# Two feed-forward weights made ternary on GpSimd instead of VectorE, in a gated cross-attention block

## What is computed

```python
def act_quant(x):
    scale = 127.0 / jnp.clip(jnp.max(jnp.abs(x), axis=-1, keepdims=True), 1e-05)
    return jnp.clip(jnp.round(x * scale), -128, 127) / scale
def weight_quant(w):
    scale = 1.0 / jnp.clip(jnp.mean(jnp.abs(w)), 1e-05)
    return jnp.clip(jnp.round(w * scale), -1, 1) / scale
def bit_linear(x, w):                       # value of: act_quant(x) @ weight_quant(w).T
...
h = bit_linear(x, w1)                       # 256 -> 1024
h = depthwise_conv1d(h, conv_w, conv_b)     # three taps along the sequence
return bit_linear(jax.nn.silu(h), w2)       # 1024 -> 256
...
x = x + tanh(g_xattn) * xattn(layernorm(x), ctx, ctx, Wq, Wk, Wv, Wo)
x = x + tanh(g_ffn)   * ffn(layernorm(x), w1, conv_w, conv_b, w2)
```

## Time and profile before

| what | value |
|---|---|
| median of 3 runs | 236.85 us (235.79 to 237.44) |
| span of the profiled execution | 235.2 us |
| TensorE busy in the span | 215.8 us (92%) |
| VectorE busy | 190.4 us (81%) |
| ScalarE busy | 161.9 us (69%) |
| GpSimd busy | 122.2 us (52%) |

### The profile page before, as it was taken

The page is one execution under the profiler, slowest core; times in us unless marked ns, Lnnn a source line. Parts: engine busy times, 40 slices in busy tenths (PEclk is TensorE's granted clock), DMA queues, the critical chain, the costliest instruction groups (busy, mean ns, idle before and its releaser), DMA issues.

```text
span 235.2 us, 6424 instructions
## 1 busy us (share of the span) xinstructions
PE 215.8 (92%) x2439; PEld 180.1 (77%) x2452; DVE 190.4 (81%) x387; ACT 161.9 (69%) x318; POOL 122.2 (52%) x229
## 2 busy tenths in 40 slices
PE   7999999997999999999999999989985699997974
PEld 7887787886878787887878878768783588886963
DVE  4163548789798999999999999999899859999671
ACT  2557768777687888989889788667933356674741
POOL 2421326364365757668677576657567224433470
PEclk9999999999999999999999999999999589999999
DMA  5982011010110101100000000000000000111111
GB/s 168 370 270 67 3 49 38 10 46 3 45 47 3 46 3 45 40 11 22 3 3 3 3 0 3 1 3 0 3 0 0 24 25 22 47 46 45 49 52 60
DMA packets 9488, 9.86 MB, mean 42 GB/s; under 512 B 1010, under 2 KB 9202, under 8 KB 9458
## 3 DMA queue, kind: packets, MB, share of 16 engines
q1 hardware_dynamic: 9458, 9.46, 12.2%
HBM read 7.36 MB, written 2.10 MB: 40 GB/s over the span
## 4 chain that ended last, share of the span: by engine, by line
PE 68%; DVE 21%; issue 5%; ACT 3%; DMA 1%; POOL 1%; SPq 0%; ACTq 0%; DVEq 0%; POOLq 0%
PE ps_score L464 10%; PE ps_proj L430 8%; PE ps_proj L509 6%; PE ps_av L487 6%; PE ps_max L474 6%; PE ps_proj L422 5%; DVE zmax L1151 5%; PE ps_proj L413 4%; PE ps_h L568 4%; PE ps_av L707 4%; DVE y L1041 4%; DVE y L1044 3%; DVE smax L987 3%; PE ps_av L497 2%; PE ps_proj L401 2%
## 5 line engine op out<-in xcount | busy, mean ns | idle before, releaser
L987 DVE TENSOR_REDUCE smax<-ps_max 128x8 f32<-128x1024 f32 x31 | 37.9, 1223 | 13.9 <-PE ps_max L474 10.7
L789 ACT ACTIVATE prob<-ps_score 128x1024 f32<-128x1024 f32 x32 | 32.7, 1023 | 17.8 <-PE ps_score L464 16.9
L464 PE MATMUL ps_score<-Qs,KT 32*128 32x128 f32 x512 | 37.1, 283 | 2.0 <-DVE smax L987 0.8
L464 PEld LDWEIGHTS ps_score<-Qs,KT 32*128 32x128 f32 x512 | 31.3, 186 | 9.3 <-issue 5.0
L474 PE MATMUL ps_max<-KT,QT 32*128 32x256 f32 x248 | 35.1, 400 | 0.0
L359 POOL TENSOR_SCALAR zq<-y,zmax 128x1024 f16<-128x1024 f32 x16 | 17.9, 1119 | 29.1 <-issue 18.1
L1151 DVE TENSOR_REDUCE zmax<-y 128x1 f32<-128x1024 f32 x16 | 19.4, 1214 | 5.3 <-ACT y L935 5.3
L336 POOL TENSOR_SCALAR xn<-xn,qa 128x256 f32<-128x256 f32 x16 | 8.1, 508 | 28.1 <-DVE qa L1027 28.1
L829 ACT ACTIVATE y<-hid,conv 128x512 f32<-128x512 f32 x24 | 18.6, 807 | 4.3 <-DVE hid L1034 3.9
L707 PE MATMUL ps_av<-w2q,zqT 128*128 128x256 f16 x128 | 17.4, 281 | 4.3 <-ACT zqT L941 2.6
L474 PEld LDWEIGHTS ps_max<-KT,QT 32*128 32x128 f32 x248 | 21.1, 184 | 0.1
(11 more groups left out here) (140 smaller groups left out, 551.9 us busy)
## 6 DMA issues: line engine op xcount, KB each, us to landing
cin<-ctxT SPq DMA_DIRECT2D x16, 128.0 KB, 2.1
xres<-x SPq DMA_DIRECT2D x16, 128.0 KB, 2.5
out<-xres SPq DMA_DIRECT2D x16, 128.0 KB, 1.7
w1f<-w1T SPq DMA_DIRECT2D x1, 1024.0 KB, 6.2
w2f<-w2T SPq DMA_DIRECT2D x1, 1024.0 KB, 8.1
wk<-wkT SPq DMA_DIRECT2D x1, 256.0 KB, 2.8
wv<-wvT SPq DMA_DIRECT2D x1, 256.0 KB, 4.4
wq<-wqT SPq DMA_DIRECT2D x1, 256.0 KB, 4.6
```

Source lines behind the costliest of these rows:

```text
L464: mm = pe.matmul(ps_score[:, i * 512 + j * P:i * 512 + (j + 1) * P], KT[b % 3][rows, j * P:(j + 1) * P], Qs[rows, j * P:(j + 1) * P], star ...
L789: act.activation(prob[pair][:, :], ps_score[:, :], ACT.Exp, scale=DH ** -0.5).then_inc(exp_done, 1)
L987: dve.tensor_reduce(dst, first_max(n, pair)[:, :].rearrange("p (g t e k) -> p g t e k", g=PG, t=KD, e=2), AX.X, ALU.max).then_inc(max_done, 1)
```

## The change

The three instructions of each piece move from VectorE to GpSimd and are put differently: scale and add 12582912 (rounds), limit to 12582911 and 12582913, and subtract 12582912 into the narrow type. In steps 3 to 6, GpSimd does one piece after `norm2` and ahead of the even tile's dequantising and `round1`, and the other at the end of its step, after `norm1` and `x_mean`. On VectorE, nothing stands in their place, and `weight_scale(1)` in step 4 follows directly on `quantise1`. ScalarE, TensorE and SyncE are not touched.

```diff
--- before.py
+++ after.py
@@ -361,12 +361,28 @@
                 gp.tensor_scalar(zdeq[:, v:v + 1], zmax[:, 4 * v + 1:4 * v + 2], w_deq[:, 0:1], None,
                                  ALU.mult).then_inc(zdeq_done, 1)
 
+            def ternary(k, wf, wt, i, step_done, done):
+                n = KD * HID // PIECES
+                wf, wt = wf[:, k * n:(k + 1) * n], wt[:, k * n:(k + 1) * n]
+                gp.wait_ge(scale_done, i + 1)
+                gp.tensor_scalar(wf, wf, w_scale[:, i:i + 1], ROUND, ALU.mult, ALU.add).then_inc(step_done, 1)
+                gp.wait_ge(step_done, 2 * k + 1)
+                gp.tensor_scalar(wf, wf, ROUND + 1.0, ROUND - 1.0, ALU.min, ALU.max).then_inc(step_done, 1)
+                gp.wait_ge(step_done, 2 * k + 2)
+                gp.tensor_scalar(wt, wf, -ROUND, 1.0, ALU.add, ALU.mult).then_inc(done, 1)
+
             norm1(0)
             norm1(1)
             x_mean(2)
+            first = (w1f, w1q, 0, wq1_step, w1q_done)
+            second = (w2f, w2q, 1, wq2_step, w2q_done)
+            pieces = {3: (0, first), 4: (2, first), 5: (0, second), 6: (2, second)}
             for s in range(NB):
                 if seq(s - 2):
                     norm2(s - 2)
+                if s in pieces:
+                    k, weight = pieces[s]
+                    ternary(k, *weight)
                 for T in TILES.get(s, ()):
                     if on_gp(T):
                         dequantise(T)
@@ -377,6 +393,8 @@
                 if seq(s + 3):
                     gp.wait_ge(sh1_done, s + 3)
                     x_mean(s + 3)
+                if s in pieces:
+                    ternary(k + 1, *weight)
             gp.wait_ge(deq_done, 1)
             norm2(NB - 2)
             quantise2(0)
@@ -1044,16 +1062,6 @@
                 dve.scalar_tensor_tensor(y3[:, :, 0:P - 1], h3[:, :, 1:P], conv[:, 4 * c + 2:4 * c + 3],
                                          y3[:, :, 0:P - 1], ALU.mult, ALU.add).then_inc(conv_done, 1)
 
-            def ternary(k, wf, wt, i, step_done, done):
-                n = KD * HID // PIECES
-                wf, wt = wf[:, k * n:(k + 1) * n], wt[:, k * n:(k + 1) * n]
-                dve.wait_ge(scale_done, i + 1)
-                dve.tensor_scalar(wf, wf, w_scale[:, i:i + 1], 1.0, ALU.mult, ALU.min).then_inc(step_done, 1)
-                dve.wait_ge(step_done, 2 * k + 1)
-                dve.tensor_scalar(wf, wf, -1.0, ROUND, ALU.max, ALU.add).then_inc(step_done, 1)
-                dve.wait_ge(step_done, 2 * k + 2)
-                dve.tensor_scalar(wt, wf, ROUND, None, ALU.subtract).then_inc(done, 1)
-
             def remainder(d):
                 dve.wait_ge(hi_done, d - LAST + 1)
                 dve.tensor_tensor(last_half(xsT_lo, d), ps_xsT.rearrange("p (k n) -> p k n", n=P),
@@ -1128,19 +1136,12 @@
                 if i == 1:
                     dve.tensor_scalar(w_deq[:, 0:1], w_mean[:, 1:2], gate[:, 1:2], None, ALU.mult).then_inc(deq_done, 1)
 
-            def pieces(first, *weight, scale=None):
-                def part(k):
-                    ternary(first + k, *weight)
-                    if scale is not None and k == 1:
-                        weight_scale(scale)
-                return part
-
             step(2, lambda k: weight_scale(0) if k == 1 else None)
-            step(3, pieces(0, w1f, w1q, 0, wq1_step, w1q_done))
-            step(4, pieces(2, w1f, w1q, 0, wq1_step, w1q_done, scale=1))
-            step(5, pieces(0, w2f, w2q, 1, wq2_step, w2q_done))
+            step(3)
+            step(4, lambda k: weight_scale(1) if k == 1 else None)
+            step(5)
             dve.wait_ge(small_in, 16)
-            step(6, pieces(2, w2f, w2q, 1, wq2_step, w2q_done))
+            step(6)
             for s in range(SB + 3, NB - 1):
                 step(s)
             last_step()
```

## The result

The changed kernel takes 244.23 us (median of 4 runs, 243.91 to 244.78) where the kernel before took 236.62 (4 runs in the same session): ratio 1.032, 95% interval 1.029 to 1.035. The forecast was 246.4 us with a range of 241.5 to 250.5. The profiled execution took 243.91 us with a span of 242.0 us, so 1.9 us lie around the span. The added loss on the span is 6.8 us. A ratio here leaves out executions more than 1.5% above the fastest of their kernel, which is one execution, in run 2.

A forecast was written before the change was run, and what follows sets the result against it. TensorE, busy 37.78 of 39.80 us in steps 3 to 6, was taken as the limit. Span: -1.06 + 3.75 + 4.1 + 2.8 = +9.6 us on 235.2, plus 1.65 for the median: 246.4 us, range 241.5 to 250.5.

The forecast's parts named there:

- The gain: Step 4: TensorE's wait at `project_out` for the second weight's mean goes, 1.06 us gained.
- The price of a piece: On GpSimd, a ternary piece of three 128x512 instructions takes 2.26 us, between bounds of 1.65 and 4.1 us.
- The rival of dear instructions: GpSimd's instructions near the two-input rate, 3.3 us a piece: +15.8 us, 252.6 us; chance 0.06.
- ScalarE's copy in step 5: The first weight's copy waits for the fourth piece until 61.3 us, so `project_q` on TensorE stalls 3.75 us.
- The rivals with cheap and dear pieces: Pieces of 1.65 us give 240.4 us, chance 0.08; pieces of 3.3 us give 252.6 us, chance 0.06.
- Step 7: TensorE waits 1.65 us at `x_transpose`, then for the last piece at `w2_column_sums`: 4.1 us late in all.
- The share of the taps: Step 7: GpSimd slows beside VectorE's convolution taps, 0.4 us at each of two places; without it 3.3 us late.
- The clock: TensorE's granted clock drops once, after the 3.8 us without work in step 5, costing 2.8 us.
- two falls: Rival: the clock drops twice, the second time in step 7: +12.4 us, 249.2 us; chance 0.27.
- The sum: Whole span: -1.06 + 3.75 + 4.1 + 2.8 = +9.6 us, giving a span of 244.8 us.
- Nothing gives the loss back: Behind step 7, TensorE is the limit through the steps, so the loss stays.
- The rival of the Trainium skill's price: GpSimd at 769 ns for 512 elements: a piece 2.6 us, the total about 2 us higher; no chance given.

The follow-up runs named there:

- run 2: The changed kernel with the column sums of the second weight moved from step 7 to step 8: 240.55 us, ratio 1.015.
- run 4: The kernel before, all pieces on VectorE, with the second weight's mean and scale computed ahead of the fourth ternary piece: 235.55 us, ratio 0.996.
- run 9: The changed kernel with the arithmetic of before on GpSimd (scale and limit, limit and round, subtract): 261.65 us, ratio 1.107.
- run 1: The changed kernel with ScalarE's two copies of the first weight moved from steps 5 and 6 to 6 and 7: 240.77 us, ratio 1.018.
- run 5: The changed kernel with spare matmuls in TensorE's two long waits, 12 in step 5 and 8 in step 7: 241.57 us, ratio 1.023.
- run 3: The changed kernel with both ScalarE's copies of the first weight and the second weight's column sums one step later: 236.26 us, ratio 0.999.
- run 6: The changed kernel with only the second weight on GpSimd, the first on VectorE, scale ahead of the fourth piece: 241.31 us, ratio 1.021.
- run 7: The changed kernel with only the first weight on GpSimd, the second on VectorE, scale ahead of the fourth piece: 240.72 us, ratio 1.017.
- run 8: The kernel before with the scale ahead of the fourth piece and 12 spare matmuls in the longest wait after the last step: 233.18 us, ratio 0.987.
- run 10: The changed kernel with copies and sums one step later, and the second weight's last two pieces split over steps 6 and 7: 236.84 us, ratio 1.001.
- run 11: The kernel of run 10 with 12 spare matmuls in the longest wait after the last step: 235.00 us, ratio 0.993.
- run 12: The kernel of run 8 with 20 spare GpSimd instructions appended, ten pairs of operations on a 128x512 tile, each twice: 260.14 us, one run.

## Why the prediction held, step by step

- **The gain** of 1.06 us for the mean of the second weight: the wait is gone and step 4 is 1.14 us shorter. Run 4 shows that this is the whole of it.
- **The price of a piece**, 2.26 us from the rows on both sides of its size: 2.1 to 2.2 us (0.69, 0.61, 0.62 with the gaps). This was right partly by luck. The rows that it came from were all pairs of arithmetic operations, and I applied them to a pair of limits. Had the pair been a mixed one, as in run 9, the same working would have been 1.3 us off for each instruction. The rival of dear instructions stopped at 3.3 us a piece, too low for that.
- **ScalarE's copy in step 5**: right in its mechanism (run 1). The wait on TensorE was 3.02 us, not 3.75, mostly because the fourth piece ended at 60.44 us, not 61.25. One step of the working was wrong here: it had GpSimd late at `round1`, with piece 2 ending at 55.75 us, 0.5 us behind the reciprocal from VectorE. That piece ended at 55.08 us, and `round1` still waited 0.18 us for VectorE. `x_mean` then ended at 58.35 us, no later than before (58.65), and the fourth piece 2.1 us behind it. So the first three pieces fitted into idle time, and the copy is late by one piece, not by a chain of three. The rivals with cheap and dear pieces, which count three in this chain, have it too sensitive to the price of a piece.
- **Step 7**: right in its mechanism and its two places (run 2 for the sums). The waits were 1.32 + 2.10 = 3.4 us against 4.1. The share of the taps, taken as 0.4 us at each of two places, was about 1.0 (L315 and L318) and 0.5 us (L372). So two errors met: without the taps' share the waits were 1.9 us where the working has 3.3.
- **The clock** is right in its total by luck. I counted one fall at 2.8 us and gave two falls a smaller chance, at 249.2 us. There were two, the second in step 7 as that rival has it, for 1.33 and 1.18 us (run 5), each less than half of what I had priced one at. The one row I had stood at half clock for 6.8 us; these were back after 3.4. One fall too few and a price twice too high cancel: 2.8 forecast, 2.5 measured.
- **The same fall differs from run to run.** The wait of 3.3 us after the last step is there in every trace of runs 1 to 11 whose kernel doesn't fill it. Where the clock stood low for 6.8 us there (before, runs 1, 6, 7, 9), the phase behind the last `project_out` takes 65.2 to 65.4 us; where it stood low for 3.4 us (after, runs 2 to 5, 10), 64.0 to 64.2; where spare matmuls filled the wait (runs 8, 11), 62.6. The trace of before is of the first kind and that of after of the second, which accounts for the 1.1 us by which the span grew less (6.8) than the start of step 8 moved (7.94). The forecast had no such term.
- **The sum.** The start of step 8 moved by -1.18 for the mean, 3.02 and 3.42 us of waits, 2.51 for the clock and 0.17 that no row names: 7.94 us. Less the 1.1 us behind the steps, the span grew by 6.8, where 9.6 was forecast. The forecast was high by 0.7 us in each of the two waits and by that 1.1; the rest is small.
- **Nothing gives the loss back** in steps 8 to 15: right, the lateness stays at 7.9 us throughout. The 1.1 us come behind them.
- **The rival of the Trainium skill's price** (GPSIMD Engine Reference, "Performance versus the Vector engine", 769 ns for 512 elements) would by the estimate in the prediction have put the total about 2 us above the forecast, near 248.5 us. The two instructions in place took 612 to 694 ns here. The runs agree with its advice under "When to use GPSIMD" to keep elementwise work on VectorE: the best kernel here (run 8, 233.18 us) leaves the ternary pieces there. No run moves GpSimd's other elementwise work.

What stays open: what decides between a clock that falls at a wait of 3 us and one that doesn't, and between one that is back after 3.4 us and one that takes 6.8.

## What to carry to other kernels

When work moves to a less busy engine, look at who waits for its last piece, and at what is queued in order behind that waiter. The 52% busy share told nothing of it, and the two waiters, both on engines that the change doesn't touch, cost 8 us; moving them one step later left some 0.7 to 0.9 us of the loss. Before moving work to relieve an engine, try first to reorder on it: here one wait held all the gain. And on GpSimd write a `tensor_scalar` on single precision tiles like these as two arithmetic operations or two limits, not one of each.

## What the runs showed of the hardware that I had not expected

- GpSimd's `tensor_scalar` on 128x512 single precision takes 0.61 us (0.69 with a scale per partition) if its two operations are both arithmetic or both limits, and 1.92 us (2.01) if they are one of each (runs 9 and 12).
- The granted clock can fall in one execution and hold in another at the same wait of 3.02 us (the changed kernel and run 2), and in the traces it stood low for 3.4, 6.8 or (run 9, behind 6.0 us of waiting) 10.2 us. The kernel before shows it in its own times: in the session of runs 1 to 4, it took 234.3 to 234.6 us in the two executions with a mean clock of 1.00, 235.7 to 236.3 at 0.991 to 0.993, and 236.8 to 237.4 at 0.983 to 0.985. In step 7 it fell behind 1.32 and 2.10 us of waiting with 0.65 us of work between them. Spare matmuls for most of a wait kept it at 1.00 in all three places where they were tried (runs 5 and 8), and gained 2.5 us for two of them. For the third the median fell by 2.4 us, of which the phase behind the steps shows 1.6 in the two traces (64.2 to 62.6 us); the kernel of run 4 that it is compared with had its clock low for longer in four of its ten executions.
